# Two node-sum copies for the first layer's scatter-adds instead of four, on one Trainium2 core

## The reference

```python
row, col = (edge_index[0], edge_index[1])          # row = src, col = dst
xj = node_features[col]
m0, m1 = ...                                       # message of an edge, from xj and its four attributes
msg = jnp.concatenate([m0, m1.reshape(e, 96)], axis=-1)
agg = jax.ops.segment_sum(msg, row, num_segments=n)
...                                                # u0, u1: bilinear in the node's features and agg
return node_features + upd
```

## Time and profile before

| what | us |
|---|---|
| median of 3 runs | 16068.78 |
| lowest and highest | 16061.02, 16078.45 |
| the profiled execution's own time | 16097.66 |
| its span | 16095.9 |

### The profile page before, as it was taken

The page is one execution under the profiler, slowest core; times in us unless marked ns, Lnnn a source line. Parts: engine busy times, 40 slices in busy tenths (PEclk is TensorE's granted clock), DMA queues, the critical chain, the costliest instruction groups (busy, mean ns, idle before and its releaser), DMA issues. The chain is left out here.

```text
span 16095.9 us, 224520 instructions
## 1 busy us (share of the span) xinstructions
PE 12040.7 (75%) x51382; PEld 9088.3 (56%) x51382; DVE 9655.3 (60%) x20249; ACT 5506.6 (34%) x10601; POOL 6391.6 (40%) x7200
## 2 busy tenths in 40 slices
PE   0268887888788888888677878888888787871777
PEld 0134444444465565655477777777777777760444
DVE  6236666666688888888755555555555555552333
ACT  0036666666522222222223333333233233330333
POOL 0337787778700000000055555555555555535000
PEclk9769999999877777777666666666666666665555
DMA  2147777777600000000123323332323332321000
GB/s 104 51 114 151 152 153 153 154 153 156 124 21 20 20 20 21 20 20 21 33 77 90 89 86 88 88 91 86 87 87 88 88 90 86 88 77 50 13 13 13
DMA packets 1044306, 1261.28 MB, mean 78 GB/s; under 512 B 202471, under 2 KB 865722, under 8 KB 1014266
## 3 DMA queue, kind: packets, MB, share of 16 engines
q0 software_dynamic: 395520, 458.93, 16.5%
q1 hardware_dynamic: 648706, 801.49, 15.6%
HBM read 1085.57 MB, written 443.97 MB: 95 GB/s over the span
## 5 line engine op out<-in xcount | busy, mean ns | idle before, releaser
L461 POOL DMA_INDIRECT sums<-e_total,e_place x1568 | 2483.5, 1584 | 464.8 <-issue 430.0
L129 POOL TENSOR_TENSOR e_gather_cell<-zeros 1x1 f32<-1x1 f32 x392 | 186.8, 476 | 5732.0 <-DMA e_at<-in_index 3638.2
L1519 POOL DMA_INDIRECT e_rows<-TS,e_at x1568 | 1627.4, 1038 | 464.2 <-issue 419.6
L1519 POOL DMA_INDIRECT e_rows<-TD,e_at x1568 | 1505.2, 960 | 477.6 <-issue 477.6
L1689 PE MATMUL ps<-e_val,e_q 128*128 128x168 f32 x3136 | 1049.9, 486 | 840.8 <-DVE e_val L1592 485.5
L1703 PEld LDWEIGHTS ps<-w_lv,e_dT 128*128 128x128 f32 x9408 | 1579.0, 246 | 0.0
L1574 DVE TENSOR_TENSOR e_silu<-e_silu,w_ad 128x256 f32<-128x256 f32 x392 | 166.6, 425 | 2327.9 <-ACT e_val L1797 1977.0
L1703 PE MATMUL ps<-w_lv,e_dT 128*128 128x32 f32 x9408 | 1532.7, 307 | 0.0
L598 PE MATMUL ps<-e_win,e_pick 128*128 128x448 f32 x3136 | 1350.7, 576 | 193.7 <-DVE e_u L495 138.2
L1689 PEld LDWEIGHTS ps<-e_val,e_q 128*128 128x128 f32 x3136 | 797.2, 312 | 984.3 <-issue 938.6
L1792 ACT ACTIVATE e_silu<-ps 128x256 f32<-128x256 f32 x392 | 150.2, 383 | 2987.9 <-DMA e_win<-T 2278.6
(11 more groups left out here) (391 smaller groups left out, 24565.0 us busy)
## 6 DMA issues: line engine op xcount, KB each, us to landing
e_win<-T SPq DMA_DIRECT2D x1568, 168.0 KB
TOT<-e_tot SPq DMA_DIRECT2D x392, 352.0 KB
e_row<-in_src_rows SPq DMA_DIRECT2D x98, 1024.0 KB
e_row<-in_dst_rows SPq DMA_DIRECT2D x98, 1024.0 KB
e_win<-T SPq DMA_DIRECT2D x1568, 56.0 KB
e_local<-LR SPq DMA_DIRECT2D x98, 512.0 KB
r_xT<-in_edge_attr SPq DMA_DIRECT2D x196, 256.0 KB
H<-r_h SPq DMA_DIRECT2D x196, 256.0 KB
```

Source lines behind the costliest of these rows:

```text
L129: pool.tensor_tensor(self.cell[:], z, z, ALU.add).then_inc(self.done, 1)
L461: pool.indirect_dma_start(sums[c], bass.IndirectOffsetOnAxis(ap=place[:, p, c:c + 1], axis=0), total[:, p, c, 0:MSG0], None, compute_op=AL ...
L1519: pool.indirect_dma_start(rows[:, p, x, c, :], None, table, bass.IndirectOffsetOnAxis(ap=at[:, gp, x, col:col + 1], axis=0)).then_inc(rows ...
```

## The change

COPIES becomes 2. Tile c of a step goes to table c % 2. A scatter-add for tiles 2 and 3 waits for tiles 0 and 1 of its own step, and one for tiles 0 and 1 waits for tiles 2 and 3 of the step before. Two tables are cleared instead of four. The node update loads two and adds them once; the semaphore of its loads gets 48 per tile instead of 80, and FRONT falls by the two adds.

```diff
-COPIES = 4
+COPIES = 2
...
-                            if not i.before(1):
+                            if c >= COPIES:
                                 gate(pool, k)
-                                pool.wait_ge(added[1 - p][c], i.uses(64, 16 * ((r + 1) // 2)))
+                                pool.wait_ge(added[p][c - COPIES], i.uses(64, 16 * (r // 2 + 1)))
+                            elif not i.before(1):
+                                gate(pool, k)
+                                pool.wait_ge(added[1 - p][c + COPIES], i.uses(64, 16 * ((r + 1) // 2)))
                             settle(pool, i.n(4, c))
-                            pool.indirect_dma_start(sums[c], bass.IndirectOffsetOnAxis(ap=place[:, p, c:c + 1], axis=0),
+                            pool.indirect_dma_start(sums[c % COPIES], bass.IndirectOffsetOnAxis(ap=place[:, p, c:c + 1], axis=0),
                                                     total[:, p, c, 0:MSG0], None, compute_op=ALU.add
                                                     ).then_inc(added[p][c], 16)
...
-FRONT, BACK = 38, 14
+FRONT, BACK = 36, 14
...
                 def sum_up(v, h, p):
                     gate(dve, k)
-                    dve.wait_ge(here[p], 80 * h + 80)
+                    dve.wait_ge(here[p], 48 * h + 48)
                     v(dve.tensor_tensor(a[:], ag[:, p, 0, :], ag[:, p, 1, :], ALU.add))
                     v(dve.tensor_copy(xd[:].rearrange("n (i u) -> n i u", i=3),
                                       xt[:, p, S:X].rearrange("n (i u) -> n i u", i=3)))
-                    v.sync()
-                    v(dve.tensor_tensor(a[:], a[:], ag[:, p, 2, :], ALU.add))
-                    v.sync()
-                    v(dve.tensor_tensor(a[:], a[:], ag[:, p, 3, :], ALU.add))
                     v.mark("summed")
```

## The result

The changed kernel takes 16,499.3 us (16,488.7 to 16,508.6, four runs), the kernel before beside it 16,064.9: **+434 us** (slower), ratio 1.0273, 95% interval 1.0256 to 1.0291. I forecast +352 and 16,420.

A forecast was written before the change was run, and what follows sets the result against it. POOL, near its own floor in the first layer's edge stage, was taken as the bound. Edge stage +478, clearing -51 and node update -75 gave +352 us, forecast 16420 us; range 16,190 to 16,670 us.

The forecast's parts named there:

- Two scatters then take 3.69 + 0.80 = 4.49 us: First layer's edge stage: landing 3.69 plus POOL restart 0.80 per two scatters, where 3.72 was taken; quiet step 8.98 us.
- I take 0.6: First layer's edge stage: late landings in busy stretches add 0.6 us per step, giving a step of 9.6 us.
- -51: Clearing before the edge stage: two fewer of four copies to zero, on the path, saves 51 us.
- -75: Node update: sum ready 0.80 us earlier per tile, 68 us over 85 tiles or 80 over 100; taken as -75.
- nothing gained: Node update: in tiles where DVE waits for PE, the shorter sum may gain nothing; PE waits in 85 of 100.
- Three times 1.86 and one of 2.2 is 7.8: Edge stage before the change: POOL's floor is 7.8 of 8.38 us per step, the other 0.6 being waiting.
- ACT's wait for landings should shrink: Edge stage: what ACT waited for hides behind POOL, as the other loop takes only 8.2 us per step.
- the landing that fits within 2.88 us: Rival, chance 0.07: scatters land before POOL reaches the new wait, step stays 8.38 us, total 15,943 us.
- Bursts hidden: Rival, chance 0.15: busy edge stretches fall into waits there anyway, step 8.7 to 9.0 us, total 16,147 us.
- Bursts counted twice: Rival, chance 0.12: both interleaved scatter chains meet both broadcast loads, 1.2 us per step, step 10.2, total 16,656 us.

The follow-up runs named there:

- the run with one scatter in flight: Kernel before with its four tables, but each scatter-add waits for the landing of the one just before: +3,838 us.
- the last experiment: Kernel before with four tables and old wait, clearing hidden behind a load, node-update adds split into two reductions: -214 us, ratio 0.9849.

## Why the prediction was right

The direction, the mechanism and the range held; the number was 79 us low. Two of its errors partly cancel: the edge stage grew by 145 us more than forecast, the node update gave back 55 us more.

- *"Two scatters then take 3.69 + 0.80 = 4.49 us"*: measured 4.34 to 4.44, and a quiet step 8.8 to 9.0 for 8.98. Both were on rows of before: ACT's release gave the landing, POOL's row after an idle spell the restart. The small excess may be ACT's own wake-up, which stands in the 3.69: quiet landings that the traces list are 3.5 to 3.7 us.
- *"I take 0.6"* for busy stretches is the term that was mis-sized. It measured 0.99 (9.97 - 8.98), 153 us more over the stage. I had counted the two broadcast loads and two thirds of one landing; half of the lateness has other sources, the radial network's loads among them.
- *-51* for the clearing: measured 51.0.
- *-75* for the node update was low by 55: 0.91 us per tile came where 0.80 was worked out, and nine fewer late tiles came on top. I had bounded the late tiles at "nothing gained", when a shorter chain could also make them rarer.
- *"Three times 1.86 and one of 2.2 is 7.8"* misreads its own row, which has 2.32 over the step's boundary: 7.9, and 0.5 us of waiting. Steps of 7.7 us in the kernel before lie under either. No term of the sum hangs on it.
- *"ACT's wait for landings should shrink"* was wrong: it grew from 651.4 to 1445.5 us. My account, from these waits: with POOL slower, ACT, DVE and PE run ahead until the two buffers of sums are full, and ACT then waits there. The wait is longer and costs nothing: places are ready before POOL comes to them, as the 34.5 us of waiting for them show.
- The rivals: the landing that fits within 2.88 us fell with the first quiet pair. Bursts hidden fell with the 9.97. Bursts counted twice had 1.2 us per step; the truth lay between it and the forecast. By the fit of the Trainium skill, "DMA: Bandwidth & Descriptors", section "Anatomy of one DMA", the scatter would have landed within about 2.2 us, an estimate from the page. Counted from the start of POOL's instruction, the run with one scatter in flight does not agree, at 3.5 us in the median; counted from the end of that instruction's 1.55 us it is about 2.0.

## What to carry to other kernels

A wait for a DMA's landing in an in-order queue costs landing plus restart, here 3.5 + 0.8 us, divided by the number in flight; it is free only if that quotient stays under the issue interval with the latest landings of the stage, not the quiet ones. Read the landing off whoever is released by it, and the busy landing off the same row in a stretch with the big loads. Before giving up parallel copies to save their clearing and summing, price the three apart: here both savings were to be had without touching the copies.

## What was not expected of the hardware

- Two-operand adds of 128x192 on POOL took 2.57 us each beside DVE's work, and DVE's products beside them took 1.40 to 1.60 us on average instead of 1.22.
- The same second layer's edge stage ran at a granted clock of 0.65 on the first chip and 0.89 on another, and whole runs of the kernel before differ between chips: 16,065, 15,846, 14,214 and 14,182 us. The edge stage of the first layer, bound by POOL and landings, took 8.34 to 8.38 us per step on the three of them where it was traced.
- One row of each, over the second layer's edges, the kernel before on the first chip and the last experiment on the other:

```profile
8400.00:14000.00 5600.00, 4518.59 (x22190) 4163.27 (x22189) 2982.13 (x6622) 1712.03 (x3096) 2914.97 (x3096) 0.65 0.30 88
```

```profile
8400.00:12000.00 3600.00, 3146.18 (x20460) 2912.42 (x20459) 2751.07 (x6108) 1577.77 (x2855) 2819.43 (x2856) 0.89 0.43 126
```
